# Token blocks of an attention and mixture-of-experts layer: second gate in one split product, statistics a block sooner, decayed keys and queries later, a longer TensorE loop

## The reference

```python
x = x + attn(layernorm(x))     # 16 heads of 32, chunks of C = 64 tokens
x = x + ffn(layernorm(x))      # router, 64 experts (8 per token, 256 slots each), one shared expert

# attn
q, k, v = proj(Wq, bq), proj(Wk, bk), proj(Wv, bv)
gate  = sigmoid(silu(x @ Wg1 + bg1) @ Wg2 + bg2)     # Wg1: 512 x 16, Wg2: 16 x 512
alpha = 0.9 * gate + 0.1
intra = softmax(causal(q k^T / sqrt(32))) v          # within a chunk
inter_t = q_t S;  S = alpha_t * S + k_t v_t^T        # a running state per head, token by token
```

## Time and profile before

| | |
|---|---|
| median of 3 runs | 4699.62 us (4697.8 to 4702.13) |
| the profiled execution's own time | 4707.31 us |
| its span in the profile | 4705.4 us |
| token stage, first to last `positions` | 133.3 to 3774.0 us of the span |
| busy over the span | PE 95%, DVE 75%, ACT 48%, POOL 28% |
| mean granted clock | 0.982 of 2.4 GHz |

### The profile page before, as it was taken

How to read it: one execution, slowest core, us unless ns; L and a number is a source line. 1 busy time by engine, 2 the same in 40 slices (tenths; PEclk the granted TensorE clock), 3 DMA queues, 4 the chain that set the end, 5 groups by cost and what they waited for, 6 DMA issues and landing times. The chain is left out here.

```text
span 4705.4 us, 183217 instructions
## 1 busy us (share of the span) xinstructions
PE 4477.3 (95%) x74416; PEld 3897.4 (83%) x74416; DVE 3518.8 (75%) x7639; ACT 2271.9 (48%) x7475; POOL 1334.0 (28%) x1275
## 2 busy tenths in 40 slices
PE   6999999999999999999999999999999969999998
PEld 5888888888888888888888888888888859999998
DVE  5777777777777777777777777777777768888887
ACT  4444444444444444444444444444444436666665
POOL 2111111111111111111112121211111146666666
PEclk9999999999999999999999999999999979999999
DMA  2000000101000000000000000001000069999997
GB/s 66 31 31 31 31 31 31 36 31 36 28 34 31 31 31 31 31 31 31 31 31 31 31 31 31 31 31 35 31 31 31 31 207 268 270 268 265 267 271 193
DMA packets 195054, 358.52 MB, mean 76 GB/s; under 512 B 16736, under 2 KB 92896, under 8 KB 194352
## 3 DMA queue, kind: packets, MB, share of 16 engines
q1 hardware_dynamic: 160848, 269.47, 16.9%
q0 software_dynamic: 33632, 79.73, 7.8%
HBM read 243.87 MB, written 107.50 MB: 75 GB/s over the span
## 5 line engine op out<-in xcount | busy, mean ns | idle before, releaser
L589 ACT ACTIVATE PR<-PR,MX 128x64 f32<-128x64 f32 x2048 | 682.6, 335 | 811.6 <-DVE MX L1171 811.6
L475 POOL TENSOR_TENSOR RI<-PV,AL 128x512 f32<-128x512 f32 x65 | 78.5, 1208 | 2540.0 <-DVE PV L1125 2540.0
L727 PE MATMUL bank<-XTh,wsguh 128*128 128x256 f32 x1536 | 447.0, 291 | 0.0
L1663 PE MATMUL ebank<-XH,WH 128*128 128x256 f32 x1536 | 431.2, 281 | 6.8 <-DVE XL L1745 6.8
L728 PE MATMUL bank<-XTl,wsguh 128*128 128x256 f32 x1536 | 430.4, 280 | 0.0
L729 PE MATMUL bank<-XTh,wsgul 128*128 128x256 f32 x1536 | 430.4, 280 | 0.0
L1663 PE MATMUL ebank<-XH,WL 128*128 128x256 f32 x1536 | 429.7, 280 | 0.0
L1663 PE MATMUL ebank<-XL,WH 128*128 128x256 f32 x1536 | 429.5, 280 | 0.0
L589 ACT ACTIVATION_READ_ACCUMULATOR PR<-PR,MX 128x1 f32 x2048 | 383.0, 187 | 0.0
L1738 DVE TENSOR_TENSOR WL<-WS,WH 128x768 fp32r<-128x768 f32 (+1 forms) x455 | 370.5, 838 | 16.2
L1600 ACT ACTIVATE WH<-WS 128x768 fp32r<-128x768 f32 (+1 forms) x455 | 325.3, 747 | 26.3 <-DMA WS<-in_L_ffn_w_down_dram 26.3
(11 more groups left out here) (228 smaller groups left out, 13456.6 us busy)
## 6 DMA issues: line engine op xcount, KB each, us to landing
WS<-in_L_ffn_w_gate_dram SPq DMA_DIRECT2D x65, 768.0 KB
WS<-in_L_ffn_w_up_dram SPq DMA_DIRECT2D x65, 768.0 KB
WS<-in_L_ffn_w_down_dram SPq DMA_DIRECT2D x65, 768.0 KB
norm_rows<-XR SPq DMA_DIRECT2D x64, 576.0 KB, 3.1
X<-in_L_attn_x_dram SPq DMA_DIRECT2D x66, 512.0 KB, 3.6
out_dram<-X SPq DMA_DIRECT2D x64, 512.0 KB, 2.9
CR<-token_counts,count_at POOLq DMA_INDIRECT x136
XG<-norm_rows,row_at POOLq DMA_INDIRECT x132, 6.4
```

Source lines behind the costliest of these rows:

```text
L475: nc.gpsimd.tensor_tensor(inverse[:, :, 0:half], PV[:, :, :], running[:, :, HC:half:-1], ALU.mult).then_inc(folded.sem, 1)
L589: ins = nc.scalar.activation(PR[b][:, j, :], PR[b][:, j, :], ACT.Exp, bias=MX[b][:, j:j + 1], scale=1.0, accum_out=SU[b][:, j:j + 1])
L727: nc.tensor.matmul(out, sh, mh, start=first, stop=False)
L1663: last = nc.tensor.matmul(bank[HID[m]][:, a * CAP:(a + 1) * CAP], w, x[odd][:, c, :], start=(c == 0 and i == 0), stop=(c == KC - 1 and i = ...
```

## The change

- `gate2` becomes one f32r matmul per part. The 16 rows of `Wg1`, `bg1` and `Wg2` are loaded three times, to rows 0, 32 and 64. `s1` is rounded to `sg` (f32r) by ACT (`s1_high`), rows 32 to 63 are then replaced by the remainder on DVE (`s1_low`); of `wg2`, rows 64 to 95 hold the remainder. One pass over the 128 rows sums the three split products.
- `X` has one buffer instead of two, and `X2` two instead of one. `X2` is loaded by a DMA of its own with the same rows of `x`; `residual` adds to it in place. `norm1`, `rstd1` and `shift1` run for block t+3 instead of t+2, `normalise` (t+2) moves into the middle of ACT's block.
- POOL starts `unpair` only after the last `softmax_b`, does both `rstd2`, and starts `decayed_k` only after both `norm2`.
- New orders on all engines, and `route_b` is cut in two (`route_rows` last). PE's loop holds eight blocks instead of four.

```diff
-BANK_OF = {"G1": 3, "Qa": 0, "G2a": 2, "G2b": 3, "Ka": 0, "Qb": 1, "Kb": 2, "ATr0": 3, "V0": 0, "V1": 1, "ATr1": 2,
-           "X2Ta": 3, "X2Tb": 0, "KTok0": 2, "RL": 1, "KTok1": 3, "GU0": 2, "RLT": 1, "GU1": 0, "GU2": 3, "DK": 1,
+BANK_OF = {"G1": 3, "Qa": 0, "Ka": 0, "G2a": 2, "G2b": 3, "Qb": 1, "Kb": 2, "ATr0": 3, "V0": 0, "V1": 1, "ATr1": 2,
+           "X2Ta": 3, "X2Tb": 0, "RL": 1, "KTok0": 2, "KTok1": 3, "GU0": 2, "RLT": 1, "GU1": 0, "GU2": 3, "DK": 1,
...
-        wg2 = sb("wg2", [GP, DIM])
+        wg2 = sb("wg2", [GP, DIM], f32r)
...
-            sp.dma_start(wg1_f[:, :, 0:GH], Wg1.rearrange("(c p) n -> p c n", p=P)).then_inc(weights_in, 16)
-            sp.dma_start(wg2[0:GH, :], Wg2).then_inc(weights_in, 16)
+            for at in COPIES:
+                sp.dma_start(wg1_f[:, :, at:at + GH], Wg1.rearrange("(c p) n -> p c n", p=P)).then_inc(weights_in, 16)
+                sp.dma_start(wg2_f[at:at + GH, :], Wg2).then_inc(weights_in, 16)
+                sp.dma_start(b1[at:at + GH, :], bg1.rearrange("(p o) -> p o", o=1)).then_inc(weights_in, 16)
...
-                sp.wait_ge(x2_ready.sem, t.value(x2_ready))
-                    load_x(Turn(t.pair, t.odd + 2))
+                if more:
+                    sp.wait_ge(out_stored.sem, t.value(out_stored, back=1))
+                    load_x2(t.next())
+                sp.wait_ge(xn_ready.sem, t.next(2).value(xn_ready))
+                load_x(Turn(t.pair, t.odd + x))
...
             with pool.Fori(0, NBLK // 2) as pair:
                 for odd in range(2):
                     t = Turn(pair, odd)
+                    pool.wait_ge(p_ready.sem, t.value(p_ready))
                     unpair(t.next())
                     fold(t.next())
+                    rstd2(t, 0)
+                    rstd2(t, 1)
+                    pool.wait_ge(x2n_ready.sem, t.value(x2n_ready))
                     decayed_k(t.next())
-                    rstd2(t, 0)
                     decayed_q(t.next())
-                    rstd2(t, 1)
-                    rstd1(t.next(2))
+                    rstd1(t.next(3))
...
+            def s1_high(t):
+                act.wait_ge(s1_made.sem, t.value(s1_made))
+                act.wait_ge(g2_filled.sem, t.value(g2_filled, back=1))
+                nc.scalar.activation(sg[:, :], s1[:, :], ACT.Copy).then_inc(s1h_ready.sem, 1)
...
+                    gate1(n)
                     exp(t, 0)
-                    gate1(n)
                     q_evac(n, 0)
+                    s1_high(n)
...
                     ot(t, 1)
+                    normalise(t.next(2))
                     exp(t, 3)
...
-            with nc.Fori(0, NBLK // 2, 2, engines=[pe.engine], hint_back_edge=True) as pair:
-                for odd in range(4):
+            with nc.Fori(0, NBLK // 2, 4, engines=[pe.engine], hint_back_edge=True) as pair:
+                for odd in range(8):
...
                     scores(t, 1)
+                    project(t, 0, wk, k_filled, ("Ka", "Kb"), parts=(0,))
                     gate2(t, 0)
                     gate2(t, 1)
                     turn_probs(t, 0)
-                    project(t, 0, wk, k_filled, ("Ka", "Kb"), parts=(0,))
+                    project(t, 0, wk, k_filled, ("Ka", "Kb"), parts=(1,))
                     outputs(t, 0)
-                    project(t, 0, wk, k_filled, ("Ka", "Kb"), parts=(1,))
...
                     outputs(t, 1)
+                    scores(t, 3)
+                    turn_probs(t, 2)
                     project(t, 1, wk, k_filled, ("Ka", "Kb"), parts=(0,))
-                    scores(t, 3)
                     turn_out(t, 0)
-                    values(t, 0, chunks=(0,))
-                    turn_probs(t, 2)
+                    values(t, 0, chunks=(0, 1))
+                    outputs(t, 2)
                     project(t, 1, wk, k_filled, ("Ka", "Kb"), parts=(1,))
-                    outputs(t, 2)
-                    values(t, 0, chunks=(1,))
...
-                    values(t, 1, chunks=(0, 1))
+                    values(t, 1)
                     x2t(t, 0)
-                    values(t, 1, chunks=(2, 3))
                     x2t(t, 1)
+                    xt(t.next(2), 0)
+                    xt(t.next(2), 1)
+                    router(t)
                     ktok(t, 0)
-                    router(t)
                     ktok(t, 1)
                     gate_up(t, 0)
                     turn_logits(t)
                     gate_up(t, 1)
-                    xt(t.next(2), 0)
-                    xt(t.next(2), 1)
                     gate_up(t, 2)
...
                     softmax_a(t, 0)
                     state(t, (0, 1))
+                    silu1(n)
                     softmax_b(t, 0)
-                    silu1(n)
+                    s1_low(n)
                     softmax_a(t, 1)
...
                     softmax_b(t, 2)
-                    inverse(n, 1)
                     softmax_a(t, 3)
                     weights(t, 2)
-                    residual(t, 0)
+                    inverse(n, 1)
                     softmax_b(t, 3)
                     weights(t, 3)
-                    norm2(t, 0)
+                    residual(t, 0)
                     values(n, 0)
                     residual(t, 1)
+                    norm2(t, 0)
                     norm2(t, 1)
                     values(n, 1)
                     x2t_low(t)
-                    norm1(t.next(2))
-                    shift1(t.next(2))
+                    norm1(t.next(3))
+                    shift1(t.next(3))
```

More of the change, by code:

```diff
@@ L33 @@
 GH = 16
+COPIES = (0, 32, 64)
 GP = 128
@@ L154, in phase_tokens @@
         b2h = sb("b2h", [P, KC])
-        X = [sb(f"X{i}", [P, NT, DIM]) for i in range(2)]
+        X = sb("X", [P, NT, DIM])
         st1 = sb("st1", [P, NT, 6])
@@ L167, in phase_tokens @@
         s1 = sb("s1", [GP, TB])
+        sg = sb("sg", [GP, TB], f32r)
         AL = sb("AL", [P, KC, NS * PAD])
@@ L190, in phase_tokens @@
         OTs = [sb(f"OTs{i}", [P, KC, P]) for i in range(2)]
-        X2 = sb("X2", [P, NT, DIM])
+        X2 = [sb(f"X2{i}", [P, NT, DIM]) for i in range(2)]
         st2 = sb("st2", [P, NT, 6])
@@ L369, in _, with turn @@
                 sp.dma_start(dst[:, :], src.rearrange("(c p) -> p c", p=P)).then_inc(weights_in, 16)
-            sp.dma_start(b1[0:GH, :], bg1.rearrange("(p o) -> p o", o=1)).then_inc(weights_in, 16)
             sp.dma_start(bvb[:, :], bv.rearrange("(o n) -> o n", o=1).to_broadcast([P, DIM])).then_inc(weights_in, 16)
-            load_x(Turn(0, 1))
-            block_counts = counts_dram.rearrange("(e n) t -> n e t", n=NBLK)
-            def turn(t, last):
-                sp.wait_ge(x2_ready.sem, t.value(x2_ready))
-                if last:
-                    sp.dma_start(X[t.buf][:, :, :], x_rows[0, :, :, :]).then_inc(x_loaded.sem, 16)
-                else:
-                    load_x(Turn(t.pair, t.odd + 2))
+            load_x2(Turn(0, 0))
+            for t in (Turn(0, 0), Turn(0, 1)):
+                sp.wait_ge(xn_ready.sem, t.value(xn_ready))
+                load_x(t.next())
+            sp.wait_ge(w_low, len(staged) + 2)
+            block_counts = counts_dram.rearrange("(e n) t -> n e t", n=NBLK)
+            def turn(t, more=True, x=3):
+                if more:
[3 more added lines that the diff above has]
+                load_x(Turn(t.pair, t.odd + x))
                 sp.wait_ge(rows_ready.sem, t.value(rows_ready))
@@ L385, in turn @@
                 sp.wait_ge(out_ready.sem, t.value(out_ready))
-                sp.dma_start(out_rows[t.pair * 2 + t.odd, :, :, :], X2[:, :, :]).then_inc(out_stored.sem, 16)
+                sp.dma_start(out_rows[t.pair * 2 + t.odd, :, :, :], X2[t.buf][:, :, :]).then_inc(out_stored.sem, 16)
                 sp.wait_ge(counts_ready.sem, t.value(counts_ready))
                 sp.dma_start(block_counts[t.pair * 2 + t.odd, :, :], CT[t.buf][:, :]).then_inc(counts_stored.sem, 16)
-            with sp.Fori(0, NBLK // 2 - 1) as pair:
+            with sp.Fori(0, NBLK // 2 - 2) as pair:
                 for odd in range(2):
[L392 to L396, removed]
+                    turn(Turn(pair, odd))
+            end = NBLK // 2 - 2
+            turn(Turn(end, 0))
+            turn(Turn(end, 1), x=0)
+            turn(Turn(end, 2), x=0)
+            turn(Turn(end, 3), more=False, x=0)
+            sp.wait_ge(x2_loaded.sem, 16 * (NBLK + 1))
+            sp.wait_ge(x_loaded.sem, 16 * (NBLK + 4))
             sp.wait_ge(rows_stored.sem, 16 * (NBLK + 1))
@@ L519, in _ @@
             rstd1(Turn(0, 1))
+            rstd1(Turn(0, 2))
             with pool.Fori(0, NBLK // 2) as pair:
@@ L638, in _ @@
             nc.scalar.activation(rwT[:, :, 0:E], bank[0][:, 0:KC * E].rearrange("p (a b) -> p a b", a=KC), ACT.Copy).then_inc(rw_ready, 1)
+            nc.scalar.activation(wg2[:, :], wg2_f, ACT.Copy).then_inc(rw_ready, 1)
             nc.scalar.mul(b1h[:, :], b1[:, :], 0.5).then_inc(rw_ready, 1)
@@ L655, in _ @@
             gate1(t)
```

(7 more changed lines are left out.)

54 lines of the change are left out of this document (32 added, 22 removed).

## The result

The changed kernel takes 4740.72 us (median of 4 runs, 4732.83 to 4748.99), the kernel before 4700.82 beside it: a ratio of 1.0086, 95% interval 1.0062 to 1.011. It is **40 us slower**. I had predicted 4642.6 with a range of 4580 to 4700; both miss.

A forecast was written before the change was run, and what follows sets the result against it. PE's list of work was taken to set the pace, its waits short apart from loop turns. Loop -47, block -19 and start +9 sum to -57 us: 4642.6 against the median of 4699.62, range 4580 to 4700.

The forecast's parts named there:

- The loop of eight, -47: PE's loop: 7 turns instead of 15, each turn priced at 5.9 us, 47 us less.
- Rival C: PE's loop: a turn of eight blocks costs twice one of four, so only the block counts: 4690; chance 0.13.
- The gate, 0.5 us for 1.8, none of it arriving: Second gate on PE: four f32r matmuls, 1.3 us less, all lost in the wait at outputs(1).
- rival F: Second gate on PE: the f32r product takes the old 1.80 us, outputs(1) 1.3 us later: 4726; chance 0.04.
- The walk through the block: One block followed through PE, DVE, ACT and POOL: it ends at T + 55.7 instead of 55.97.
- the term of 19 us: Token stage: each block 0.3 us shorter, 19 us less in all; bounds 19 slower to 115 faster.
- the wait at outputs(1): PE at outputs(1) waits some 1.8 us for DVE's weights, starting at T + 19.1 where it started at 18.91.
- rival E: PE at outputs(1): the clock falls to 1.2 GHz after the new wait in every block, 154 us: 4796; chance 0.05.
- Holding the keys, "nothing": POOL's KD, started at norm2's end (36.1), ends at 38.5, 0.4 us before ktok reads it; cover called thin.
- rival D: POOL line 512: KD comes late, ktok and gate_up(0) start 2.1 us late, 134 us: 4776; chance 0.06.
- The start, +9: Ahead of PE's first transpose: six more small loads on SP's queue, 7.2 us, plus DVE work; 9 us more.
- Rival B: Unit 1's exp and softmax_b come sooner; PE's 1.8 us a block arrive: 4547, with half 4604; chance 0.12.

The follow-up runs named there:

- fill: Changed kernel with the first half of the second key projection moved on PE ahead of outputs(1), no work added: 4661.71 us, ratio 0.9917.
- fill and spread: Changed kernel with half the second key projection moved ahead of outputs(1) and a query half put between outputs(0) and scores(2): 4610.01 us, ratio 0.9819.
- scores spread: Changed kernel with half a projection on PE between outputs and the scores behind them (units 0/2 and 1/3): 4746.34 us, ratio 1.0106.

## Why the prediction was wrong

- **The loop of eight, -47:** right. -49 and -47 in the two kernels. Rival C (a turn costs twice) is out for a loop of eight.
- **The gate, 0.5 us for 1.8, none of it arriving:** right; rival F is out. It arrives, 1.3 us in each block without a turn, once the wait is filled.
- **The walk through the block:** right in every station named above to 0.3 us, 55.98 for 55.7, but only where the clock holds. The 0.3 us a block that it was to gain (the term of 19 us) did not arrive: 55.98 for 55.95. As the time of *every* block it was wrong: the 56 blocks without a turn take 57.5 us on average, where the 48 before take 56.3.
- **Where the step failed: the wait at outputs(1) was priced by its length alone.** I saw that 1.8 us of idle would stand in each block and dismissed a fall of the clock behind it (rival E, 0.05), because a wait of 1.2 us in the rows of before had left the clock alone. That was one wait, 1.23 us at 113.8 us of the span, ahead of the loop; it was shorter, and it says nothing of 64 longer ones. The length was right: 71 us at the outputs and 47 in the stalls inside blocks, for 64 x 1.8 = 115. What stood at nothing was the clock. E happened, at about its price, in 22 blocks, behind the whole wait, and not in all 64; 11 more falls stand behind the stall in scores(2), ahead of outputs(1), and 6 in blocks with the turn. Together that is 178 us of half clock, about 89 us lost, by an estimate that takes half of it. My stage was to last 3640.7 - 47 - 19 = 3575 us and lasts 3678, 103 more; the clock is most of that, and the 19 us that did not arrive are most of the rest.
- **What wasn't in the prediction at all:** outputs directly followed by scores. I priced new neighbours as switches of kind and counted their joins only as gains. 64 and 96 small matmuls in a row have an "issue" wait in them, of 0.4 to 1.2 us in the blocks shown. That it adds to the loss is shown ("fill" against "fill and spread", 52 us); that PE there runs out of fetched instructions is only argued, from the fact that nothing on the chip ends these waits, that they stand at the same matmul in every pass of the loop, and that large matmuls in between remove most of them. The Trainium skill, "Runtime: NRT & Kernel Launch", section "Instruction fetch mechanics", holds that fetching in a straight run is mostly hidden; if these waits are fetching, here it isn't, and no run shows that they are.
- **Holding the keys, "nothing":** wrong in its reason. KD does end in time (it starts at T + 36.8 in the block at 2237.45, forecast 36.1), and rival D is out. But with the keys ahead of the powers x2t is late: 66 us. I costed the moved step by its own lateness and not by what used to stand behind it on POOL's queue.
- **The start, +9:** PE's first scores start 2.0 us later (75.3 for 73.3), the first `positions` 3.7; in that first block the clock fell once more, from 102.6 us on. The six added loads take 3.3 us on SP's queue, where I had priced them at 7.2 by the longer ones ahead of them.
- **Rival B (waits shrink)** needed the exps sooner; the walk excluded it. "Fill and spread" comes near its 4604 (4610) in another way, by giving PE the wait as working time.

Open: why the clock falls behind some waits of one length and not behind others (22 of 27 in the changed kernel, 33 of 56 in "scores spread", 6 of 27 at x2t), and what the "issue" stalls are. How much of the loss is the clock is an estimate from the half clock; in no run does the clock alone change.

## What to carry to other kernels

A wait that a change opens on the engine that sets the pace costs its length only if the clock stays. Before such a wait is priced by its length, look for waits as long, with the same neighbours, in a trace; one shorter wait is no evidence. Where large matmuls can be moved into it, move them, even where the same work stood a microsecond behind. In this kernel, with the wait filled, two bursts of small matmuls next to each other cost 52 us more than with large ones between, and a burst behind the loop's turn 22 to 30 more than large ones there. When an order is moved, cost each queue by who stood *behind* the moved step, too.

## What the runs showed of the hardware

- The granted clock fell to 0.50 behind 1.43 to 1.45 us of idle that had small matmuls behind it, in 22 of 27 blocks of the changed kernel and 33 of 56 of "scores spread"; behind 1.67 to 1.70 us with small ones ahead of it in 28 of 28; behind 1.41 to 1.56 us with large ones on both sides in 6 of 27; and it held behind 0.80 us in the middle of small ones.
- A turn of PE's loop has no fixed price: 1.67 and 2.46 us of idle and about 5 us of half clock with small matmuls behind it, one stall of 0.9 to 1.8 us at the turn with 12 more matmuls in each block of the loop, 0.6 to 1.3 us with the clock held when large matmuls follow, and 3.1 to 3.7 us with half clock when they follow and the loop holds 16 blocks.
- More work in a wait can be free: 1.4 us added to each block, and the 56 blocks without a turn no longer (57.4 us on average for 57.5).
